# Second gather of a graph layer: one signal per two pairs, a load lead of 11 pairs, row numbers in quarters, transposes ahead of the closing products

## The reference, cut to what matters

```python
x = x + gnn(layernorm(x), W, src, dst, edge_weight)      # x: (6250, 256), 100000 edges
x = x + ffn(layernorm(x), gate_w, ...)                   # 16 experts, the best 2 of each row

def gnn(x, W, row, col, val):
    h = einsum('nd,od->no', x, W)
    return segment_sum(val[:, None] * h[col], row, num_segments=6250)
```

## Time and profile before

| | us |
|---|---|
| median of 3 runs | 2196.22 (2194.57 to 2212.91) |
| the profiled execution | 2194.18 |
| its span in the profile | 2192.4 |
| second gather, 604 to 1609 us of the span | 1005.0 |
| POOL busy in it | 618.3 |
| TensorE busy in it | 654.0 |
| VectorE busy in it | 273.3 |

### The profile page before, as it was taken

How to read it: one execution, slowest core, us unless ns; L and a number is a source line. 1 busy time by engine, 2 the same in 40 slices (tenths; PEclk the granted TensorE clock), 3 DMA queues, 4 the chain that set the end, 5 groups by cost and what they waited for, 6 DMA issues and landing times. The chain is left out here.

```text
span 2192.4 us, 33976 instructions
## 1 busy us (share of the span) xinstructions
PE 1521.2 (69%) x7875; PEld 1191.4 (54%) x7876; DVE 976.2 (45%) x2548; ACT 642.5 (29%) x1788; POOL 1206.6 (55%) x1170
## 2 busy tenths in 40 slices
PE   6165977775655766666666577766436999998975
PEld 4164766553334544444444344544325998897864
DVE  6997898863322222222222422223164333333348
ACT  5661266641000111110110111011053444443455
POOL 0025658776666666666666656665532555554435
PEclk9596679886678878887888788887659999999988
DMA  5122322223633223222222222222363223225356
GB/s 169 51 71 61 90 60 69 64 74 98 211 105 92 83 83 87 87 86 82 85 86 86 82 77 85 88 85 78 76 155 135 69 71 104 86 81 180 104 166 230
DMA packets 121466, 215.63 MB, mean 98 GB/s; under 512 B 21000, under 2 KB 82755, under 8 KB 121280
## 3 DMA queue, kind: packets, MB, share of 16 engines
q0 software_dynamic: 52864, 140.45, 21.9%
q1 hardware_dynamic: 53664, 56.14, 7.8%
q10 hardware_dynamic: 14880, 18.35, 2.6%
HBM read 172.32 MB, written 42.54 MB: 98 GB/s over the span
## 5 line engine op out<-in xcount | busy, mean ns | idle before, releaser
L473 POOL DMA_INDIRECT hbuf<-xn_rows,ix x640 | 618.3, 966 | 375.1 <-issue 173.2
L556 PE MATMUL bank<-hbuf,picks 128*128 x1640 | 536.2, 473 | 340.6 <-SPq L461 193.7
L556 PEld LDWEIGHTS bank<-hbuf,picks 128*128 128x128 f32 x1640 | 351.2, 232 | 519.0 <-issue 470.9
L498 DVE TENSOR_SCALAR picks<-iota_two,marks 128x256 f32<-128x256 f32 x640 | 247.9, 434 | 726.3 <-remote 420.6
L744 POOL DMA_INDIRECT fbuf<-xn_rows,first_tables x196 | 235.8, 1203 | 122.6 <-PE bank L1269 54.7
L634 ACT ACTIVATE agg<-bank 128x256 f32<-128x256 f32 x49 | 18.8, 383 | 763.3 <-remote 579.3
L1853 PE MATMUL bank<-rowsT,w_sb 128*128 128x128 f32 x1744 | 215.8, 277 | 18.9 <-issue 18.9
L1853 PEld LDWEIGHTS bank<-rowsT,w_sb 128*128 128x128 f32 x1744 | 211.6, 193 | 31.1 <-issue 26.6
L1789 POOL DMA_INDIRECT expert_out<-y_sb,to_i x112 | 111.1, 992 | 189.9 <-DVE y_sb L1898 185.4
L1863 PE MATMUL bank<-w_sb,hT 128*128 128x256 f32 x872 | 207.7, 381 | 0.6 <-ACT hT L1811 0.4
L1287 PE MATMUL bank<-work 128*128 128x192 bf16 x1568 | 161.0, 261 | 62.7 <-DVE work L1075 50.3
(11 more groups left out here) (294 smaller groups left out, 1721.7 us busy)
## 6 DMA issues: line engine op xcount, KB each, us to landing
w_sb<-in_L_ffn_w_dram ACTq DMA_DIRECT2D x28, 512.0 KB
hbuf<-xn_rows,ix POOLq DMA_INDIRECT x640
first_sums<-x SPq DMA_DIRECT2D x49, 128.0 KB
first_sums_back<-first_sums SPq DMA_DIRECT2D x7, 896.0 KB
xn_rows<-xn SPq DMA_DIRECT2D x7, 896.0 KB, 4.6
x<-in_x_dram SPq DMA_DIRECT2D x6, 896.0 KB
ya<-expert_out SPq DMA_DIRECT2D x5, 896.0 KB, 5.6
yb<-expert_out SPq DMA_DIRECT2D x5, 896.0 KB, 7.5
```

Of the source, the lines that this page charges most:

```text
L473: pool.indirect_dma_start(hbuf[:, 1 + j, k, :], None, xn_dram, bass.IndirectOffsetOnAxis(ap=ix[:, 2 * j + k:2 * j + k + 1], axis=0)).then_ ...
L498: s = v.tensor_scalar(picks[:, j % 2, k, :], iota_two[:], marks[:, 0, 2 * j + k:2 * j + k + 1], marks[:, 1, 2 * j + k:2 * j + k + 1], ALU. ...
L556: m = nc.tensor.matmul(bk[q][:, 0:D], picks[:, j, k, q * P:(q + 1) * P], hbuf[:, ds(place + j, 1), k, :].rearrange("p s d -> p (s d)"), st ...
```

## The change

Four edits, all in the second gather. POOL's lead grows from 6 pairs to 11. TensorE counts `used` up by two with the last product of a quad, instead of by one with the last product of each pair. The row numbers are copied in four parts of 8 columns a ring instead of two of 16, the last part of a ring at j = 2 and the first three parts of the next ring at j = 6, 10 and 14; POOL waits for each part. And `turn` and `project` move from behind the closing quad to ahead of it.

```diff
-        AHEAD = 6
+        AHEAD = 11
...
-        HALF = GR // 2
+        PART = PR // 4
+        NUMBERS = 2 * PART

         def number(v, i, h):
-            v.tensor_copy(ix[:, h * HALF:(h + 1) * HALF], dst_i[:, ds(i * GR + h * HALF, HALF)]).then_inc(ix_set, 1)
+            v.tensor_copy(ix[:, h * NUMBERS:(h + 1) * NUMBERS], dst_i[:, ds(i * GR + h * NUMBERS, NUMBERS)]).then_inc(ix_set, 1)
...
-                    if j % (PR // 2) == 0:
-                        pool.wait_ge(ix_set, i * 2 + (j // (PR // 2) + 1))
+                    if j % PART == 0:
+                        pool.wait_ge(ix_set, i * 4 + (j // PART + 1))
                     await_turn(pool, used, i, PR, j + 1 + PR - ahead)
...
                     if j == 2 and not isinstance(i, int):
-
                         await_turn(dve, pair_in, i, PR, 0)
-                        number(v, i, 1)
-                    if j == PR // 2 + 2:
-                        await_turn(dve, pair_in, i, PR, PR // 2)
-                        number(v, i + 1, 0)
+                        number(v, i, 3)
+                    if j > PART and j % PART == 2:
+                        await_turn(dve, pair_in, i, PR, j - 2)
+                        number(v, i + 1, j // PART - 1)
...
                 with pe.Fori(first, end, 2) as s:
                     for m in quad(s, q):
-                        m.then_inc(used, 1)
-
-                for m in quad(end, q):
-                    pass
-                m.then_inc(closed, 1)
+                        pass
+                    m.then_inc(used, 2)
+
                 if not isinstance(w, int) or w >= 1:
                     turn(w - 1, 1 - q)
                 if not isinstance(w, int) or w >= 2:
                     project(w - 2, q)
+                for m in quad(end, q):
+                    pass
+                m.then_inc(closed, 1)
...
-                number(v, 0, 0)
-                number(v, 0, 1)
+                for h in range(4):
+                    number(v, 0, h)
```

## The result

The changed kernel takes 2250.98 us (median of 4 runs, 2241.26 to 2270.39) against 2200.51 of the kernel before in the runs beside it (2194.57 to 2212.91): ratio 1.0246, 95% interval 1.0203 to 1.0288. It is slower; the forecast was 2188, 0.4% faster, and the time lies 1 us past the range's upper end.

What follows compares the result with a forecast made beforehand. It saw a loop of signals with no engine full and one POOL pause per window; signals +8, transposes -12 and numbers -4 gave -8 us, 2194.2 to 2186.2, plus 2.0 to the median: 2188, range 2080 to 2250.

Steps and rivals of the forecast that it cites:

- a lead that only moves where the credit ends: POOL's lead of 11 pairs in the second gather: 0 per window, 0 in all.
- Transposes ahead: Turn and project before the closing quad: 0 in forty windows, -12 us in nine; bounds -68 and 0.
- nine windows: Windows taken to have four loop quads, where the chain itself is waited for: +8 us for signals, -12 for transposes.
- Numbers in quarters: Row-number copies on VectorE: 0 in the rings, -4 us in the last ring, bounds -12.7 and 0.
- 0.9 later per quad: With one signal per quad, picks wait for both pairs, so a quad ends at 859.0 instead of 858.10.
- no wait, 0 in a window of three loop quads: The quad's signal has 4.0 us to arrive before POOL's credit ends and needs 2.0, so POOL loses nothing.
- about 865.2: End of the next window's first quad, instead of 866.39, still before POOL's last load ends at 867.89.
- with no cover: Upper bound of the signal term if POOL's string does not hide the later quads: +88 us.
- The second pause: Rival: late quad signals stop POOL twice a window; +50 us, 2238, in a third of 46 windows; chance .17.
- Prompt signals: Rival: fewer TensorE signals come in time and the boundary's pause closes; -96.6 us, 2091; chance .32.
- Numbers that hold POOL: Rival: number copies sit behind late picks on VectorE, so the lead misses 11; +41 us, 2229; chance .07.
- fewer signals change nothing: If TensorE's multiplication itself drags on while POOL issues, halving its signals gains nothing; time is the sum's, 2188.

Runs made afterwards that it cites:

- lead_alone: The kernel before with the lead of 11 pairs and the numbers in quarters, signals per pair, transposes behind the closing quad: 1.0034 of before.
- turns_alone: The kernel before with one edit, transpose and projection ahead of the closing quad: 0.9944 of before.
- signals_alone: The kernel before with one edit, `used` counted up by two with a quad's last product: 1.0163 of before.
- signals_undone: The changed kernel with `used` counted up once per pair again: 1.0006 of the kernel before.

## Why the prediction was wrong

**What bounds the kernel, and the lead.** The reading held: a loop of signals, strings of twelve loads, one pause a window, and a lead that only moves where the credit ends. lead_alone is within 1% (1.0034), with loads in 985 us against 989.5. That a longer lead "buys time for landings, of which little is lacking" held.

**Transposes ahead.** Priced at -12 us; turns_alone gave -0.56%, 12 us. The size was right (the interval spans 4 to 20 us), but it was booked on nine windows and is not shown to lie there, so that is luck as far as the runs tell; in the changed kernel it is not seen.

**Numbers in quarters.** 0 in the rings, -4 at the end; measured 16.7 us in 12 waits against 12.7 in one, +4. With a signal per pair (lead_alone) POOL waited 5.8 us in 8 places, 7 less than before: the term was about right by itself and turned its sign behind the late signals. It is small either way.

**The step that failed.** "plus 1.99 for the quad, 859.0, against 858.10. So 0.9 later per quad", and from it "no wait, 0 in a window of three loop quads". The 1.99 us came from one window in which TensorE was at the upper level. The prediction had read the granted clock of 0.81 for the stage and gave it no part in the sum. At the upper level the step was about right, 0.65 later (5.29 us against 4.64 for two quads). In the slow window, where TensorE had been idle for 6.38 us and ran at 0.50, a quad took 3.78 us, and the two quads came 4.2 later (8.82 against 4.64; 2.7 later than the kernel before with its first quad slow, 6.08). With a signal per pair picks lie beside products, and the slow quads of the kernel before lengthened no pause; with one per quad they are in line, twice a window. The next window's first quad was predicted to end at "about 865.2", 12.2 us after POOL resumed at 852.99; it ended after 11.7 us in the fast window and after 20.6 in the slow one. The margin was computed for the wrong signal, too: not the third quad's, which had 4.0 us to spare, decides, but this one, which started only when POOL's string was over (879.43), and whose 3.55 us, mostly at the low level, were added to the pause. The term was +8 us with a bound of +88 "with no cover"; signals_alone costs 1.63% of 2200, 36 us, the changed kernel against signals_undone 2.4%, 53.

**The rivals.** The second pause (2238) came near in time, but not as a mechanism: strings were not cut into eight and four as a rule (39 of twelve, 3 of eight, 4 of four), the one pause grew from 3.2 to 5 to 7 us in part of the windows. A second pause of 3.3 us and a quad at the low level in the pause happen to cost alike, so the near hit is luck. Prompt signals did not come about: with half as many, POOL's waits for TensorE and remote signals rose from 189.2 us to 236.6. Numbers that hold POOL cost 4 us, not 41.

The Trainium skill ("Perfetto Trace Analysis", section "Per-instruction lifecycle: what the profiler-reported window actually captures") was weighed with the rule that a TensorE end is an estimate. The start at 879.43, of a quad whose pairs the closing quad had already used, with 2.83 us idle and nothing shown ahead of it, suggests that TensorE's work itself is held there, not only its signals; that agrees with that reading, and no run here settles it. What the prediction drew from it, that "fewer signals change nothing", did not hold: they cost 2.4% in the changed kernel.

## What to carry to other kernels

A signal that is sent half as often also lets its receiver start later: before merging two, look at what ran beside each other between them, and price the line that results at the slower of the durations that the trace shows, not at the one in the window that was picked. Here 25 of 35 strings held products at the lower clock already in the kernel before, at no cost beside the picks: so where a stretch's mean clock is under 1 (0.81 here), the slower durations belong into the sum as soon as the work moves onto the path. And where a producer runs in strings and pauses, its mean pace is the number to look for: slowing it to that pace (here a useless fill of 1.8 us behind every fourth pair) was worth 1.5% over the same kernel without, while more lead was worth nothing.

## What was not expected of the hardware

While POOL issued a load every 1.26 us, TensorE's signals came late and so did some of its own steps, and slowing the loads made the kernel faster: at 1.48 us a load POOL's waits for TensorE and remote signals fell from 194.6 us to 27.6. Why is open. A quarter of the bytes changed nothing (985 against 989.5 us, one run). And three products of no use per quad, 0.49 us each at the upper level (1.46 for the three), took 1.7% off the changed kernel, with the clock at 0.90 instead of 0.78; two such products a quad in turns_alone took nothing off.
